# A scan and mixture-of-experts kernel: no warming steps, the weight maxima turned earlier, two GpSimd products behind the scales, group 0's pieces at new steps

## What is computed

```python
def step(state, xb_t):                       # a recurrence over the 2048 tokens
    state = tanh(state @ A.T + xb_t)         # xb = x @ B.T, 128 values
    return state, state
states = scan(step, zeros, xB)
y  = states @ C.T + D * x + x
x1 = layernorm(x + layernorm(y) * gamma + beta)
# mixture of experts: 8 experts, best 2 of the better half by sigmoid scores, and a shared expert
routed = sum_e comb[:, e] * ((silu(x1 @ w_gate[e]) * (x1 @ w_up[e])) @ w_down[e])
shared = (silu(x1 @ sw_gate) * (x1 @ sw_up)) @ sw_down
out = layernorm(x1 + routed + shared)
```

## Time and profile before

| | us |
|---|---|
| runs of the kernel | 412.38, 414.62, 414.31 |
| median | 414.31 |
| the profiled execution | 412.55 |
| its span on the core | 410.8 |

### The profile page before, as it was taken

How to read it: one execution, slowest core, us unless ns; L and a number is a source line. 1 busy time by engine, 2 the same in 40 slices (tenths; PEclk the granted TensorE clock), 3 DMA queues, 4 the chain that set the end, 5 groups by cost and what they waited for, 6 DMA issues and landing times.

```text
span 410.8 us, 7488 instructions
## 1 busy us (share of the span) xinstructions
PE 378.9 (92%) x2587; PEld 252.9 (62%) x2587; DVE 320.2 (78%) x744; ACT 138.0 (34%) x280; POOL 157.2 (38%) x149
## 2 busy tenths in 40 slices
PE   6999969859999999998999899989998999999991
PEld 5998868525566656665666566556665665555561
DVE  2343988757976999699969997999799789974564
ACT  2554213222243333432342324232424333333330
POOL 1969515013332443344234423451354125423232
PEclk9999989979999999999999999999999999999997
DMA  7970000005202801270123015501540173005211
GB/s 224 329 273 2 2 0 1 2 4 158 49 0 59 150 2 53 76 131 1 53 90 118 0 53 116 89 0 51 124 82 0 53 145 62 20 34 161 45 53 51
DMA packets 15901, 29.95 MB, mean 73 GB/s; under 512 B 1720, under 2 KB 4288, under 8 KB 15872
## 3 DMA queue, kind: packets, MB, share of 16 engines
q1 hardware_dynamic: 15872, 29.58, 27.6%
HBM read 25.24 MB, written 4.33 MB: 72 GB/s over the span
## 4 chain that ended last, share of the span: by engine, by line
issue 27%; DVE 24%; PE 22%; POOL 12%; DMA 7%; SPq 5%; ACT 2%; POOLq 1%; DVEq 0%; ACTq 0%
PE bank L382 9%; POOL h L978 9%; PE bank L452 4%; DMA xT<-comb_dram 3%; DVE st L694 3%; PE bank L295 3%; DVE xT L850 3%; SPq L208 3%; DVE xT L854 3%; POOL rstd L963 2%; PE bank L301 2%; DMA xres<-in_L_attn_x_dram 2%; DVE wu L725 2%; DMA comb_dram<-combT 1%; DVE wg L734 1%
## 5 line engine op out<-in xcount | busy, mean ns | idle before, releaser
L978 POOL TENSOR_TENSOR h<-xT,h 128x512 f16<-128x512 f32 x72 | 86.1, 1196 | 200.6 <-ACT h L579 200.6
L452 PE MATMUL bank<-wd,h 128*128 128x256 f16 x864 | 106.1, 273 | 0.9 <-DVE wd L862 0.4
L382 PE MATMUL bank<-x2T,wg 128*128 128x512 f16 x432 | 106.3, 382 | 0.0
L382 PE MATMUL bank<-x2T,wu 128*128 128x512 f16 x432 | 105.2, 380 | 0.0
L452 PEld LDWEIGHTS bank<-wd,h 128*128 128x128 f16 x864 | 84.2, 98 | 25.0 <-issue 1.6
L579 ACT ACTIVATE h<-xT 128x512 f16<-128x512 f32 x72 | 45.3, 630 | 131.8 <-DVE xT L854 128.4
L382 PEld LDWEIGHTS bank<-x2T,wu 128*128 128x128 f16 x432 | 42.3, 98 | 51.5 <-issue 0.8
L850 DVE SCALAR_TENSOR_TENSOR xT<-bank,u_un,xT 128x512 f32<-128x512 f32 x64 | 47.6, 744 | 22.5 <-ACT xT L568 21.6
L568 ACT ACTIVATE xT<-bank,g_un 128x512 f32<-128x512 f32 x72 | 49.2, 683 | 46.7 <-PE bank L382 36.5
L382 PEld LDWEIGHTS bank<-x2T,wg 128*128 128x128 f16 x432 | 41.9, 98 | 36.7 <-issue 1.4
L854 DVE TENSOR_TENSOR xT<-xT 128x512 f32<-128x512 f32 x64 | 44.3, 692 | 6.8 <-DMA xT<-comb_dram 4.9
(11 more groups left out here) (122 smaller groups left out, 352.1 us busy)
## 6 DMA issues: line engine op xcount, KB each, us to landing
xT<-comb_dram SPq DMA_DIRECT2D x64, 256.0 KB, 7.4
xres<-in_L_attn_x_dram SPq DMA_DIRECT2D x7, 512.0 KB, 6.0
out_dram<-xskip SPq DMA_DIRECT2D x7, 512.0 KB, 2.7
wd<-in_L_ffn_w_down_dram SPq DMA_DIRECT2D x1, 1024.0 KB, 6.9
xres<-in_L_attn_x_dram SPq DMA_DIRECT2D x2, 256.0 KB, 3.0
out_dram<-xskip SPq DMA_DIRECT2D x2, 256.0 KB, 2.0
B_sb<-in_L_attn_B_dram SPq DMA_DIRECT2D x1, 128.0 KB, 2.6
C_sb<-in_L_attn_C_dram SPq DMA_DIRECT2D x1, 128.0 KB
```

What stands on the lines that cost most here:

```text
L382: last = pe.matmul(ps[:, :], w[:, pw, e, m // 3, :], x2T[:, par, px, m // 3, :], start=(m == 0), stop=(m == NUP // 2 - 1))
L452: return pe.matmul(ps_y[t // 2][:, (t % 2) * DM:(t % 2 + 1) * DM], h16[:, e % 3, ph, t * P:(t + 1) * P], wd16[:, pw, e, :], start=start, s ...
L978: nc.gpsimd.tensor_tensor(h16[:, e % 3, 1, :], h[:, b, :], h16[:, e % 3, 0, :], ALU.subtract).then_inc(h_low, 1)
```

## The change

The warming pass is gone: the first pass starts from zeros, and there are 64 steps in place of 68. The x tiles are taken in order 0 to 7, where tile group 7 came first. The maxima are turned at s = 21 and spread at s = 23, while the loads of x are still being turned. `scales()` has one step fewer: the floor of 2^-60 now goes into the diagonal with a scalar_tensor_tensor (from a new `tiny_diag`), and the mask reads the bank. GpSimd's last two products wait for `wstep` to reach 9, the end of `scales()`. DVE does split 3 before group 0's pieces, and the pieces have new steps.

```diff
--- before.py
+++ after.py
@@ -25,7 +25,7 @@
     KT = DM // P
     L = NB * S // P
     NCH = P // NB
-    WARM = 4
+    WARM = 0
     T4 = 4
     G = L // T4
     GT = T4 * P
@@ -82,6 +82,7 @@
         wmax = sb("wmax", [P, 5])
         wmax_row = sb("wmax_row", [5, 1])
         wmax_diag = sb("wmax_diag", [5, 5])
+        tiny_diag = sb("tiny_diag", [5, 5])
         ones = sb("ones", [5, P])
         wpow = sb("wpow", [P, 5])
         wscale = sb("wscale", [P, 5])
@@ -140,7 +141,7 @@
         fb_mm, fb_tanh, fb_kept = sem("fb_mm"), sem("fb_tanh"), sem("fb_kept")
         skip_done, res_done = sem("skip_done"), sem("res_done")
         wmax_part, wmax_turned, wmax_step, wmax_known = sem("wmax_part"), sem("wmax_turned"), sem("wmax_step"), sem("wmax_known")
-        wstep, weights_ready = sem("wstep"), sem("weights_ready")
+        wstep, weights_ready, tiny_made = sem("wstep"), sem("weights_ready"), sem("tiny_made")
         w_high = [sem(f"w_high{i}") for i in range(5)]
 
         def ahead_sems(prefix):
@@ -166,7 +167,7 @@
         out_dram = out.rearrange("b s d -> (b s) d").rearrange("(p l) d -> p l d", l=L)
 
 
-        chunks = [L // T4 - 1] + list(range(L // T4 - 1))
+        chunks = list(range(L // T4))
         pairs = [c * T4 // 2 + j for c in chunks for j in range(T4 // 2)]
 
         WEIGHT_LOADS = [
@@ -182,10 +183,10 @@
         HALVES = 2 * (len(pairs) - FIRST)
 
 
-        PE_AT = {1: (0, 0), 2: (0, 1), 10: (1, 0), 11: (1, 1), 26: (4, 0), 27: (4, 1), 28: (5, 0), 29: (5, 1),
-                 30: (6, 0), 31: (6, 1)}
-        ACT_AT = {27: 5, 29: 6, 31: 7}
-        UP_FROM = 31
+        PE_AT = {1: (0, 0), 2: (0, 1), 8: (1, 0), 9: (1, 1), 23: (4, 0), 24: (4, 1), 26: (5, 0), 27: (5, 1),
+                 29: (6, 0), 30: (6, 1)}
+        ACT_AT = {25: 5, 28: 6, 31: 7}
+        UP_FROM = 30
         WHOLE = 2
         NUP = 2 * 3 * KT
 
@@ -314,13 +315,13 @@
                 scan_step(s, tiles, seeds if s in (0, WARM) else run_state[:, (s - 1) % 2, :])
                 if s < HALVES:
                     turn_x(FIRST + s // 2, s % 2)
-                if s == WARM:
+                if s == 4:
                     turn_Cr()
-                if s == WARM + 26:
+                if s == 21:
 
                     pe.wait_ge(wmax_part, 5)
                     pe.transpose(ps_mats[0][0:5, 0:P], wmax[:, :], ident[:, :]).then_inc(wmax_turned, 1)
-                if s == WARM + 28:
+                if s == 23:
 
                     pe.wait_ge(wmax_step, 3)
                     pe.matmul(ps_mats[0][:, P:P + 5], ones[:, :], wmax_diag[:, :], start=True, stop=True).then_inc(wmax_known, 1)
@@ -617,8 +618,11 @@
             nc.vector.memset(fb_state[:, :, :], 0.0).then_inc(seed_clear, 1)
             nc.vector.memset(ones[:, :], 1.0).then_inc(wmax_step, 1)
             dve.wait_ge(AB_turned, 1)
+            dve.wait_ge(consts, 1)
             nc.vector.tensor_copy(AT[:, :], ps_mats[0][:, 0:P])
             nc.vector.tensor_copy(BT[:, :, :].rearrange("p k n -> p (k n)"), ps_mats[0][:, P:(KT + 1) * P]).then_inc(AB_done, 1)
+            nc.vector.tensor_scalar(tiny_diag[:, :], ident[0:5, 0:5], 2.0 ** -60, None, ALU.mult).then_inc(tiny_made, 1)
+            dve.wait_ge(tiny_made, 1)
             UN = 2.0 ** -WTOP / XS
 
 
@@ -640,12 +644,11 @@
                 dve.wait_ge(wmax_turned, 1)
                 nc.vector.tensor_reduce(wmax_row[:, :], ps_mats[0][0:5, 0:P], AX_X, ALU.max).then_inc(wmax_step, 1)
                 dve.wait_ge(wmax_step, 2)
-                nc.vector.tensor_scalar(wmax_diag[:, :], ident[0:5, 0:5], wmax_row[:, 0:1], None, ALU.mult).then_inc(wmax_step, 1)
+                nc.vector.scalar_tensor_tensor(wmax_diag[:, :], ident[0:5, 0:5], wmax_row[:, 0:1], tiny_diag[:, :],
+                                               ALU.mult, ALU.max).then_inc(wmax_step, 1)
                 dve.wait_ge(wmax_known, 1)
-                nc.vector.tensor_scalar(wpow[:, :], ps_mats[0][:, P:P + 5], 2.0 ** -60, None, ALU.max).then_inc(wstep, 1)
-                dve.wait_ge(wstep, 1)
-                nc.vector.tensor_scalar(wpow[:, :].bitcast(I32), wpow[:, :].bitcast(I32), 0x7F800000, None,
-                                        ALU.bitwise_and).then_inc(wstep, 1)
+                nc.vector.tensor_scalar(wpow[:, :].bitcast(I32), ps_mats[0][:, P:P + 5].bitcast(I32), 0x7F800000, None,
+                                        ALU.bitwise_and).then_inc(wstep, 2)
                 dve.wait_ge(wstep, 2)
 
                 nc.vector.tensor_scalar(wscale[:, :].bitcast(I32), wpow[:, :].bitcast(I32), -1.0,
@@ -685,7 +688,7 @@
                 dve.wait_ge(w_in[min(i, 2)], 16 * 2)
                 greatest(i)
             scales()
-            for i in (0, 1, 2):
+            for i in (0, 1, 2, 3):
                 split(i)
 
             def stats(k, g, src, st_sem, mv_sem, t0, t1):
@@ -807,13 +810,11 @@
 
 
             dve.wait_ge(res_done, 2)
-            dve.wait_ge(weights_ready, 3)
+            dve.wait_ge(weights_ready, 4)
             for e in range(E1):
                 piece(e, 0, 0, main)
                 if e == 4:
                     split(4)
-                elif e == 6:
-                    split(3)
             choose(0, main)
             weigh(0, main)
 
@@ -950,6 +951,9 @@
                                         beta_bc[:, :].unsqueeze(1).to_broadcast([P, T4, DM]), ALU.add).then_inc(res_done, 1)
 
             for n in range(L // T4):
+                if n == L // T4 - 2:
+
+                    pool.wait_ge(wstep, 9)
                 skip(n)
             pool.wait_ge(vecs_in, 16 * NVEC)
             for n in range(L // T4 - 2):
```

## The result

The changed kernel takes 421.61 us (median of 4 runs, 420.69 to 422.73) against 413.94 for the kernel before (412.38 to 414.62): a ratio of 1.019, 95% interval 1.015 to 1.023. It is slower by 7.7 us. The profiled execution took 420.69 us, with a span of 419.0; its counterpart before took 412.55, with 410.8. The branch for runs that don't meet isn't taken.

A forecast was written before the change was run, and what follows sets the result against it. It took the chain of x loads, DVE's scales, splits and norms, with DVE and GpSimd shutting each other out, as the bound; +6.1 (y1) +0.4 (clock) -0.4 (routing) = +6.1 us on 414.31 gave 420.4, range 416.0 to 424.0.

The forecast's parts named there:

- the saved steps: Second pass on TensorE: four steps fewer start it 4.1 us earlier, at 38.65, but waiting for y1 eats the gain.
- T: The turning of x1 on TensorE, at 71.63 us before; forecast to move by 6.5 us, to 78.1.
- The gain of 0.35 us: From T to the routing's start: 9.05 us instead of 9.40, since split 3 is gone from there.
- the train of splits: DVE's eight split operations after `scales()`, alternating with GpSimd's eight; first y1 forecast at 61.2, 6.1 us later.
- DVE is first by my reading: After `scales()`, DVE takes the ports before GpSimd, so its last low part waits for only seven GpSimd operations, 16.3 us.
- rival 1: After `scales()`, GpSimd gets the ports first; all eight operations precede the last low part: 2.3 us more, 422.7; chance 0.14.
- the sum of the durations: Behind `scales()`, DVE's 12.6 us and GpSimd's 18.6 us can't overlap; blocked operations save up to 1.4 us.
- TensorE's next half piece ... 0.4 us more: Second y1 behind the first: TensorE's half piece runs at the lower clock after its 15 us wait, adding 0.4 us.
- my step count: TensorE's steps followed from T to the routing's start, with pieces over eight steps instead of five: T + 9.05.
- Rival 2: Splits beside GpSimd: low parts need no turn at the ports, y1 3.8 us early, 410.4 us; chance 0.11.
- Rival 3: Splits after `scales()`: DVE keeps the ports while work is queued, +3.2 us, 417.5; chance 0.09.
- Rival 4: The first pass forgets too little from zero, the test of the runs fails, over 2100 us added; chance 0.03.

## Why the prediction was right, and which terms were off

**The mechanism and the sign.** DVE and GpSimd take turns, the alternation reaches to the first y1, the saved steps are eaten, TensorE's wait was forecast at 15 us and is 15.68, `wscale` and `wmax_diag` at 0.2 and are 0.17 and 0.21. The run with small sums shows the cause; that with the warming steps alone shows the steps to be worth nothing as long as an earlier split meets more of GpSimd's sums.

**The size.** The forecast was +6.1 us; the medians differ by 7.7, the profiled executions by 8.1. By its terms:

| term | forecast | measured |
|---|---|---|
| second pass starts at | 38.65 | 39.35 |
| `scales()` ends at | 32.9 | 33.5 |
| from there to the last split's end | 28.3 (27.5 to 28.9) | 28.9 |
| first y1 later by | 6.1 | 7.4 |
| second y1 behind the first | 3.8 | 4.14 |
| T later by | 6.5 | 8.2 |
| T to the routing's start | 9.05 (9.40 before) | 8.98 (9.31 before) |

The 9.40 was the end of split 3; the routing's first row had started at 80.94, so it was 9.31. The gain of 0.35 us forecast for this stretch is 0.33 measured.

The 1.7 us by which T was missed are 0.6 in `scales()`'s end, 0.6 in the train of splits, 0.4 in the second y1 and 0.1 in the rest. The first is not the kernel's engines: wd's reduction starts at 27.42 instead of 26.88, as its load landed later. In the other kernels with the tiles in order it started between 27.1 and 29.1; whether the order of the tiles has a part in that, or only the spread of loads from run to run, stays open, since of the kernel before there is one trace. The later start of the second pass changed nothing, as TensorE had to wait for y1 anyway.

**Two errors that partly cancel.** "DVE is first by my reading" was wrong: GpSimd went first. Its product's row starts at 33.57, 0.05 us behind DVE's at 33.52, and yet it is DVE's high part that takes 3.63 us, and all eight of GpSimd's operations stand before wd's last low part. This is rival 1 in its order, priced there at 2.3 us more. The other term was the sum of the durations: 12.6 and 18.6 us would be 31.2, and the stretch took 28.94, since a pair of a high part and a product or sum takes 3.51 to 3.63 instead of 3.74, and a pair with a low part 4.6 instead of 4.94. I had allowed at most 1.4 us for it, and it is 2.3. For the train of splits the wrong order and the undersized saving come to 28.3 us against 28.94, closer than rival 1's 30.6, and that is luck: two errors of opposite sign. In the time, rival 1's 422.7 is as close to 421.61 as the forecast's 420.4, a little closer even; of it too that says nothing, since its train was 1.7 us too long and it shares the terms that came out short. By the page "SBUF — State Buffer" of the Trainium skill, section "Who interferes with whom", the first to issue has the ports; the profile's starts, 0.05 us apart, did not tell who that was, and the engine with the earlier row waited.

**The clock.** "TensorE's next half piece ... 0.4 us more" came out as 0.76 (66.69 - 62.55 = 4.14 against 3.38): the first product took 1.22 us instead of 0.70, at a granted clock of 0.50 (62 to 64 us). Behind T, my step count held to 0.1 us. What I did not see is that this depends on where TensorE's long wait ends; the run with the later half pieces showed that.

**The rivals.** Rival 1, GpSimd first, is what happened, though priced too high. Rival 2, low parts that need no turn, is refuted: a low part takes 4.59 us beside a product, and 2.62 alone. Rival 3, DVE keeping the ports, is refuted by the same rows: in the changed kernel every part waits for one operation, never for none and never for two. Rival 4 did not occur: the test of the runs held.

## What to carry to other kernels

Work that runs beside a data wait is free only as long as the other engine doesn't need its ports; before moving port-bound work earlier, sum up both engines' time in operations that exclude each other, from that point to the first result that is waited for. That sum, not the longer of the two, is close to the time: 31.2 us by the sum here, 28.9 measured. An engine held idle so that a few small operations of another run undisturbed has to do its work later, beside big ones: some 4.8 us of idling with the data there bought 0.8 us here and cost 4.6. Put such work beside reductions, statistics, and operations that read one input from PSUM, all of which kept their durations beside it here, and if a stall can't be avoided, place it away from a stretch in which TensorE's clock is on the path.

## What the runs showed of the hardware beyond that

An operation as small as 128 x 16 waits for a whole GpSimd operation (2.30 us in place of 0.23), as a big one does, while in the kernel before the six tensor_scalars of 128 x 1 from 44.38 to 45.07 took 0.14 to 0.20 us each beside a sum. Two queued trains alternated strictly here: sixteen operations, one by one, worked out from DVE's durations and GpSimd's two sums of 5.79 and 20.72 us. A DVE operation that waited took 0.1 to 0.4 us less than its own time and the GpSimd operation's together. And the engine whose row starts first by 0.04 or 0.05 us was not the one that went first: with the high part ahead, wg's low part (start 35.13) waited for the product that started at 35.17, as at 33.52 and 33.57 in the changed kernel. Why GpSimd was first in both cases stays open.
